# Attention values written transposed in 32-column groups: no evacuation, no transposes back, sums from a block of ones

## The reference

```python
    x = x + _L0_xattn_ref(_layernorm(x, axis=-1), ctx_1024, ctx_1024, mask_BxS2_bk0, ...)
    x = x + _L0_ffn_ref(_layernorm(x, axis=-1), L0_ffn_wg1, L0_ffn_bg1, L0_ffn_wg2, L0_ffn_w_in, L0_ffn_w_out)
...
        qh, kh, vh = (split_heads(qp), split_heads(kp), split_heads(vp))
        scores = jnp.einsum('bhqd,bhkd->bhqk', qh, kh) * d_head ** (-0.5)
        ...
        attn = jax.nn.softmax(scores, axis=-1)
        out = jnp.einsum('bhqk,bhkd->bhqd', attn, vh)
        out = out.transpose(0, 2, 1, 3).reshape(b, l, d_model)
        return out @ Wo.T + bo
```

## Time and profile before

| | us |
|---|---|
| median of three runs | 765.07 |
| the profiled execution, its own time | 765.94 |
| its span, first to last instruction | 763.8 |
| attention, up to the last `values` | about 454 |
| expert stage | about 460 to 720 |
| tail | about 720 to 764 |

### The profile page before, as it was taken

One profiled execution on the slowest core, in us unless ns is written; L12 is line 12 of the kernel. 1 busy time (PEld: TensorE's weight loads), 2 busy tenths in 40 slices (PEclk: granted clock), 3 DMA queues, 4 the chain that ended last, 5 costly groups with the idle time before them and its releaser, 6 DMA issues.

```text
span 763.8 us, 14153 instructions
## 1 busy us (share of the span) xinstructions
PE 574.9 (75%) x4326; PEld 405.7 (53%) x4326; DVE 443.1 (58%) x1706; ACT 407.7 (53%) x862; POOL 359.7 (47%) x438
## 2 busy tenths in 40 slices
PE   3499999889888988898898767483778866789800
PEld 1156666556455555555465446362667755679700
DVE  4267788778777877777785773251323322223374
ACT  2257988887787888688786655230322322224300
POOL 4122126644554564455435326647555555550075
PEclk9989999999999999999998987867898999989955
DMA  3363111221122122201111224324544444446498
GB/s 89 71 195 84 45 41 44 61 67 43 50 60 66 29 65 63 66 24 30 38 29 32 83 59 122 105 77 112 158 133 124 118 125 124 120 131 186 133 364 291
DMA packets 74458, 73.59 MB, mean 96 GB/s; under 512 B 22032, under 2 KB 61840, under 8 KB 74096
## 3 DMA queue, kind: packets, MB, share of 16 engines
q1 hardware_dynamic: 64160, 53.86, 26.8%
q0 software_dynamic: 8640, 18.37, 6.8%
q10 hardware_dynamic: 1584, 0.46, 0.2%
HBM read 44.99 MB, written 27.70 MB: 95 GB/s over the span
## 4 chain that ended last, share of the span: by engine, by line
PE 53%; ACT 14%; issue 13%; DVE 7%; another core or an unknown queue 4%; POOL 4%; SPq 2%; DMA 2%; ACTq 0%; POOLq 0%; DVEq 0%
PE bank L638 12%; PE bank L649 10%; PE bank L462 6%; PE bank L484 6%; DVE sm L890 3%; PE bank L466 3%; POOL gathered L1417 3%; PE bank L475 3%; PE bank L629 3%; ACT sm L717 2%; ACT pt L782 2%; ACT vx L709 2%; ACT rows L744 2%; PE bank L491 2%
## 5 line engine op out<-in xcount | busy, mean ns | idle before, releaser
L1354 POOL DMA_INDIRECT routed_rows<-rows,pos x128 | 125.2, 978 | 136.4 <-ACT rows L746 86.2
L1390 POOL DMA_INDIRECT expert_rows_by_token<-yb,token_row x118 | 113.2, 960 | 85.7 <-DVE token_row L1248 40.8
L638 PE MATMUL bank<-xbT,wi 128*128 128x256 f32 x312 | 97.1, 439 | 71.1 <-issue 70.4
L827 ACT ACTIVATE hb<-bank 128x512 f32<-128x512 f32 x78 | 46.6, 597 | 168.7 <-PE bank L638 77.4
L1254 DVE TENSOR_TENSOR yb<-bank,gate 128x256 f32<-128x256 f32 x78 | 33.1, 424 | 172.2 <-PE bank L649 107.2
L638 PEld LDWEIGHTS bank<-xbT,wi 128*128 128x128 f32 x312 | 59.6, 212 | 84.7 <-issue 77.0
L882 DVE TENSOR_REDUCE smax<-bank 128x8 f32<-128x512 f32 x128 | 82.2, 683 | 30.7 <-PE bank L466 25.4
L649 PE MATMUL bank<-wo,hb 128*128 x624 | 91.6, 295 | 0.0
L649 PEld LDWEIGHTS bank<-wo,hb 128*128 128x128 f32 x624 | 85.3, 212 | 0.1
L462 PE MATMUL bank<-kx,qT 64*64 64x512 f32 x512 | 74.6, 654 | 14.0 <-DMA kx<-kT 7.1
L890 DVE TENSOR_TENSOR sm<-bank,smax 128x512 f32<-128x512 f32 x128 | 81.9, 681 | 0.0
(11 more groups left out here) (135 smaller groups left out, 934.8 us busy)
## 6 DMA issues: line engine op xcount, KB each, us to landing
xb<-routed_rows SPq DMA_DIRECT2D x78, 138.0 KB
wi<-w_in SPq DMA_DIRECT2D x78, 128.0 KB
kx<-expert_rows_by_token SPq DMA_DIRECT2D x26, 256.0 KB
ctx_in<-ctx_t SPq DMA_DIRECT2D x16, 256.0 KB
x_all<-x SPq DMA_DIRECT2D x16, 256.0 KB
kx<-kT SPq DMA_DIRECT2D x256, 16.0 KB
out<-x_all SPq DMA_DIRECT2D x16, 256.0 KB
expert_rows<-yb SPq DMA_DIRECT2D x19, 128.0 KB, 2.1
```

What stands on the lines that cost most here:

```text
L638: last = nc.tensor.matmul(UBK[b % 2][:, c * BLK:(c + 1) * BLK], wi[:, b % RX, c * P:(c + 1) * P], xbT[:, b % RH, :], start=True, stop=True)
L1354: nc.gpsimd.indirect_dma_start(out=rows_d, out_offset=bass.IndirectOffsetOnAxis(ap=pos[:, buf, k, u:u + 1], axis=0), in_=rows[:, buf, u, : ...
L1390: nc.gpsimd.indirect_dma_start(out=tok_d, out_offset=bass.IndirectOffsetOnAxis(ap=token_row[:, b % RY, u:u + 1], axis=0), in_=yb[:, b % RY ...
```

## The change

- `vx` becomes double by group, and each pair of adjacent value pairs lies in one row of 160 columns with zeros between, so that a window of 32 columns picks the features of one head pair for one sequence, at the place where they belong among 32 output partitions.
- `values` makes 16 matmuls of 32 stationary columns and 64 queries: for each half of a head group (j), each sequence (b) and each of four column groups (g). The four column groups write four different quarters of the partitions of `XB[:, 0:128]`. Nothing is computed for the wrong sequence. Eight more matmuls (32 columns, 128 queries) with a constant block of ones put the sum of each head on all eight of its features' partitions in `XB[:, 128:256]`.
- DVE's `normalise` takes the reciprocal of 128 x 128 sums and multiplies once, straight into `onT`, which is now double. There are no `xo`, `on`, `queries_to_rows`, `transpose_o` and `onT_evac`.
- `values(t)` newly waits for `normalise(t - 1)`, because it overwrites `XB`; `project_o(t - 1)` waits for it too. The waits that stood before `queries_to_rows` move to just before `project_o`. `v_evac` waits for an older tile's values only.
- At the start one memset of `vx` (5120 numbers per partition) takes the place of four copies of 512. The gathers of the tail use 8 buffers inside `sm` in place of 6 of their own.

```diff
-        vx = sb("vx", [P, U, J, VM])
+        vx = sb("vx", [P, 2, U * J // 2, 2, 2 * VB + 2 * DH])
...
                 def values(t, u):
+                    if t:
+                        pe.wait_ge(s_norm, t)
                     pe.wait_ge(s_ptev, 2 * t + 2)
-                    for j in range(J):
-                        o = VM * (j % 2)
-                        last = nc.tensor.matmul(XB[o:o + VM, (j // 2) * P:(j // 2 + 1) * P], vx[:, u, j, :],
-                                                pt[:, j, :], start=True, stop=True)
+                    for j in range(2):
+                        for b in range(2):
+                            for g in range(J // 2):
+                                v = vx[:, t // U % 2, u * (J // 2) + g, :, :].rearrange("p a c -> p (a c)")
+                                c = (2 * j + b) * VB
+                                nc.tensor.matmul(XB[g * VB:(g + 1) * VB, b * L:(b + 1) * L], v[:, c:c + VB],
+                                                 pt[:, 2 * g + j, b * L:(b + 1) * L], start=(j == 0 and b == 0), stop=False,
+                                                 skip_group_check=True)
+                    for j in range(2):
+                        for g in range(J // 2):
+                            last = nc.tensor.matmul(XB[g * VB:(g + 1) * VB, P:2 * P],
+                                                    ones_s[:, j * VB:(j + 1) * VB], pt[:, 2 * g + j, :],
+                                                    start=False, stop=(j == 1), skip_group_check=True)
                     last.then_inc(s_pv, 1)
-                def queries_to_rows(t):
-                    pe.wait_ge(s_xev, t + 1)
...
-                def transpose_o(t):
...
                 def project_o(t):
-                    pe.wait_ge(s_ontev, t + 1)
-                    nc.tensor.matmul(YB[:, P:2 * P], onT[:, :], wo_s[:, :], start=True, stop=True).then_inc(s_y, 1)
+                    if t:
+                        pe.wait_ge(s_res, t)
+                    pe.wait_ge(s_norm, t + 1)
+                    nc.tensor.matmul(YB[:, 0:P], onT[:, t % 2, :], wo_s[:, :], start=True, stop=True).then_inc(s_y, 1)
...
                 def v_evac(s):
                     act.wait_ge(s_v, s + 1)
+                    if runs(s, 2):
+                        act.wait_ge(s_pv, (s - 1) * U)
...
-                        act.wait_ge(s_pv, t + 1)
-                        nc.scalar.activation(xo[:, :, :].rearrange("p c q -> p (c q)"), XB[:, :], ACT.Copy
-                                             ).then_inc(s_xev, 1)
...
                 def normalise(t):
-                    dve.wait_ge(s_tq, t + 1)
-                    y = YB[:, :].rearrange("r (j m) -> r j m", m=VM)
-                    nc.vector.reciprocal(rden[:, :, :], y[:, :, 4 * DH:4 * DH + 2]).then_inc(s_rden, 1)
+                    if t > 1:
+                        dve.wait_ge(s_y, t - 1)
+                    dve.wait_ge(s_pv, t + 1)
+                    nc.vector.reciprocal(rden[:, :], XB[:, P:2 * P]).then_inc(s_rden, 1)
                     dve.wait_ge(s_rden, t + 1)
-                    for b in range(2):
...
-                    last.then_inc(s_norm, 1)
+                    nc.vector.tensor_tensor(onT[:, t % 2, :], XB[:, 0:P], rden[:, :], ALU.mult).then_inc(s_norm, 1)
...
-                for u in range(U):
-                    last = nc.vector.tensor_copy(vx[:, u, :, :], ones_s[:, :].unsqueeze(1).broadcast_to([P, J, VM]))
-                last.then_inc(s_zero, 1)
+                nc.vector.memset(vx[:, :, :, :, :], 0.0).then_inc(s_zero, 1)
```

More of the change, by code:

```diff
@@ L31 @@
 EPS = 1e-5
-VM = 64
+VB = 32
 J = H // 2
@@ L61 @@
 RL = 2 * HH // KTOP
-RG = 6
+RG = 8
 TB0 = SPS[0] * U
@@ L95, in build @@
     spread_c = nc.inline_tensor((NEG_B * np.eye(P)).astype(np.float16), name="mask_spread")
-    ones_cols = np.zeros((P, VM), np.float32)
-    for p in range(2):
-        ones_cols[p * L:(p + 1) * L, 4 * DH + p] = 1.0
+    ones_cols = np.zeros((P, 2, VB), np.float32)
+    for j in range(2):
+        for p in range(2):
+            o = (2 * j + p) * DH
+            ones_cols[p * L:(p + 1) * L, j, o:o + DH] = 1.0
+    ones_cols = ones_cols.reshape(P, 2 * VB)
     ones_c = nc.inline_tensor(ones_cols, name="value_ones")
@@ L558, in body @@
                         transpose_probs(t, u)
-                        if before:
-                            if u > 1 or runs(s, 1):
-                                pe.wait_ge(s_res, t - 1)
-                            if u == 2 and runs(s, 2):
-                                pe.wait_ge(s_lsh, s - 1)
-                            if u == 0 and runs(s, 3):
-                                pe.wait_ge(s_pch, 6 * s - 16)
-                            queries_to_rows(t - 1)
                         if u == 0 and runs(s, 0, NS - 2):
@@ L585, in body @@
                             transpose_rows(s - 2, par)
-                        if before:
-                            transpose_o(t - 1)
                         if u == 3 and runs(s, 0, NS - 2):
@@ L604, in _ @@
                     body(s, s // 2, s % 2)
-                pe.wait_ge(s_res, NT - 1)
-                pe.wait_ge(s_pos, NS - 2)
-                queries_to_rows(NT - 1)
                 transpose_rows(NS - 2, 0)
-                transpose_o(NT - 1)
                 gate_hidden(NS - 2)
-                pe.wait_ge(s_ontev, NT)
+                pe.wait_ge(s_pch, 6 * NS - 16)
                 project_o(NT - 1)
```

52 lines of the change are left out of this document (19 added, 33 removed).

## The result

The kernel after takes 806.71 us (median of 4; 802.29 to 810.34), beside 764.15 for the kernel before in the same job: ratio 1.0574, 95% interval 1.0521 to 1.0626. The forecast was 725. Two later jobs gave 1.0583 (1.0468 to 1.0698) and 1.0575 (1.0486 to 1.0663).

A forecast was written before the change was run, and what follows sets the result against it. Bound by a DVE-PE loop, ACT's stream and a hold once a group, no engine full. Gains 33 (groups 4 to 13) + 6 + 4 = 43, less 2, 41 us: 765.94 - 41 - 0.9 = 724, said as 725; range 716 to 734.

The forecast's parts named there:

- the hold: Once a group ACT and DVE wait on something remote; taken from first `pt` start to release, 5.9 us on average.
- And the hold: Release at 17.2 + 5.9 = 23.1 us still ends last, so a group's period goes from 26.4 to 23.1 us.
- rivals 2 and 3: The hold's release doesn't move with ACT's rows, 742 us (0.09); or the hold goes away, 703 us (0.07).
- rival 4: Slower: the 24 matmuls don't run side by side or issue too slowly; values 2.75 us, total 800 us; chance 0.07.
- The values on PE: New values and ones block on PE: 1.03 to 1.47 us a tile, taken as 1.05, about 1.03 before.
- rival 1: First half: 64-query passes no shorter, values 1.47 us; second: DVE's reciprocal 1.0 us. Either 736 to 740, both 748; chance 0.16.
- DVE: `normalise` on DVE: reciprocal taken as 0.65 us, whole 0.95 (0.6 to 1.3) against 0.89 before: no gain.
- Rival 2: The hold's release doesn't move with ACT's rows: 1.7 us won behind `project_v` lost, 17 in ten groups, 742; chance 0.09.
- The loop without holds: Path through DVE and PE over one group: the first projection would end at 20.9 us, before the hold's release.
- Groups 0 to 3: No hold there, PE without a gap: 0.6 us won in two or three tiles, 1.5 a group, 6 in all.

The follow-up runs named there:

- align: Kernel after, with POOL's row scatters of turns 1 and 2 waiting for that turn's values to be reported: 766.40 us, ratio 1.0036.
- b_recip: Kernel before, with an extra reciprocal of 128 x 128 numbers on DVE in each tile, into a spare buffer: 765.85 us, ratio 0.9999.
- split0: As align, and turn 0's four scatters cut into two pairs, the second behind the turn's values: 727.78 us, ratio 0.9451; again 0.9396.
- spread3_2: Rerun of kernel after with one scatter pair behind turn 0's values, one behind turn 1's, four behind turn 2's: 729.79 us, ratio 0.9589.
- run8: Kernel after, with all eight row scatters of a group issued in one run in turn 0: 833.46 us, ratio 1.0887.
- probe2: Separate program, second run: TensorE blocks beside 0 to 8 indirect scatters; first values block's report 4.8 us late with four, on time with none.
- b_s0_split16: Kernel before, row scatters moved behind the values blocks and its 8 products of values cut into 16: 652.46 us, ratio 1.0081; repeat (_2) 739.74 us, 0.9693.

## Why the prediction was wrong

The step that failed is the hold: "I take it as an interval from the group's first `pt` start to the release", and then, in *And the hold*, "The hold lets go at 17.2 + 5.9 = 23.1". It took one hold a group, at a fixed place, and asked only whether its end would move or it would vanish (rivals 2 and 3). It didn't ask what makes it, though it names the condition: it begins with POOL's scatters. The new block puts three times the instruction rows into the turns in which POOL issues its other two pairs. There the runs showed a second hold of 1.9, half clock for 1.4 and a values block 1.6 longer, all of it gone from these turns in align. No rival had a second hold, and rival 4, which ends on the right side, did so by another mechanism.

The path against the trace, with 0 at 257.77:

| | forecast | after | what lies between |
|---|---|---|---|
| scores, u = 1 | 1.53 | 1.55 | right |
| values | 3.00 | 3.11 | right |
| values and ones on PE | 1.05 | 1.02 | right |
| residual | 4.82 | 6.75 | a hold, 1.9 |
| scores, u = 2 | 6.68 | 8.72 | same |
| values, u = 2 | 8.15 | 11.60 | half clock, 1.4 |
| residual | 9.76 | 14.81 | values 2.68 for 1.05, 1.6 |
| next `pt` | 17.2 | 22.25 | same |
| release of turn 0 | 23.1 | 29.86 | also 7.6 after `pt`, not 5.9 |

The numbers behind the second half are 272.58 for the second residual, 280.02 for `pt`, 287.63 for the next residual after the hold:
```profile
272.58 0.29 DVE L890 TENSOR_TENSOR x_all<-bank,x_all 128x128 f32<-128x128 f32 x1 [2.14 <-PE bank L502]
...
287.63 0.29 DVE L890 TENSOR_TENSOR x_all<-bank,x_all 128x128 f32<-128x128 f32 x1 [2.62 <-remote]
```
```profile
280.02 1.08 ACT L772 ACTIVATE pt<-bank 128x512 f32<-128x512 f32 x2
```
```profile
281.72 0.98 POOL L1331 DMA_INDIRECT routed_rows<-rows,pos  x1 [9.50 <-DVE pos L971]
```
Every late entry lies behind a hold, the clock that falls after one, or the values that stand still beside a run. Up to the next `pt` that is 5.1; of the 1.7 of the last line 1.5 comes by POOL: its run started 0.18 after `pt` before, with ACT's rows, and 1.70 after it now, because DVE's positions come last.

*The values on PE*: right, and rival 4 and the first half of rival 1 with it wrong. The 24 matmuls take 1.02, on average 0.043 us each. The estimate of 1.49 in the prediction went by the Trainium skill's "TensorE: Matmul & The Clock Gate", section "Wait — 56ns, not 53.3ns?", whose 62 ns a MATMUL hold with hardware decode off; the trace doesn't have them, and no run tells which way of decoding was on.

*DVE*: the reciprocal took 0.94 on average where 0.65 was taken and 1.0 was the bound; `normalise` 1.17 (259.46 to 260.63) instead of 0.95. The slope between the two rows in sight was the wrong ruler, and it was misread: 0.04 / 12 is 0.0033, which gives 0.59, not 0.64. The steeper slope of the bound, 0.08 / 12, was near: 0.94 / 128 is 7.3 ns a number. The Trainium skill's "VectorE: DVE Perf Modes", section "First, the fixed hardware budget", gives the reciprocal's divide a repeat count of 8; the trace has 0.94 beside the 0.29 of a multiplication as large, 3.2 times, which fits a dearer instruction but doesn't show the count. That the reciprocal cost nothing is shown in the kernel before (b_recip); for the kernel after no run tells.

*Rival 2* took 1.7 for what is won behind `project_v`. By the prediction's own numbers it is 5.96 before (20.47 - 14.51) and 4.44 after (17.2 - 12.76), so 1.5.

*The loop without holds* was put at 20.9 a group. split0 shows 23.64, with DVE busy 277.62 of 300, that is 21.9 a group. So 20.9 was below what DVE's work alone takes; 4 x 0.22 of it is the reciprocal. A forecast for split0 by this path would have been too low by some 2.7 a group, and that 725 is near 728 is chance.

*Groups 0 to 3*: 6 us forecast, 7.1 measured (136.31 to 129.18). Right in size: 0.7 is there before the first values, then the groups win 2.2, 1.4, 2.1 and 0.6, where 1.5 each was forecast. The reason given, a PE without a gap, fits the kernel before (from 70 to 130 us PE busy 56.38 of 60). After, DVE is the fuller one (PE 54.22, DVE 55.14), so there part of PE's gain may be used up by DVE; no run parts the two.

## What to carry to other kernels

Where a profile has waits "on remote" or "on issue" that end just after a run of indirect DMAs, take them as a resource that PE's short instructions share with that run: list every run and what PE does in it, before and after the change, turn by turn. An edit that makes one matmul into three can be cheap on PE and cost 4 us a group by where it falls. And it is worth moving the runs on purpose: behind the report of the block with the most short instructions, which here took 79 of 807 us off the changed kernel and 3.8% off the one before. Then look again at what the moved run meets (in spread3_2 the projection of the values), and whether anything waits for it.

## What was not expected of the hardware

- TensorE's reports come up to 8.4 us after the modelled end of their work (run8) while GpSimd issues indirect scatters of 0.96 us each, and TensorE itself is slowed to one to six matmul rows in 0.7 us (probe2). VectorE's and ScalarE's work and reports go on meanwhile (in the kernel after DVE runs its maxima from 261.41 to 262.68, POOL being at its first scatter).
- One of the seven jobs ran on a chip that had none of it, with the same 0.96 for a scatter, and had the kernel before in 648 us where the others took 760 to 773. On it the attention of b_s0_split16 had a period of 24.21 a group, and 24.59 on the chip of b_s0_split16_2. From the last values to the end it took 228.9 there and 313.6 here, 85 of the 90 us between the two. In that part POOL scatters the experts' rows, and the kernel before waits 69.3 us in 15 waits on remote for the first product of the experts alone (its longest is 13.7):
```profile
ACT hb L827 <- remote: 69.3, 15, 13.7
```
- Moving the scatters of the attention leaves that part as it was: split0, too, has 51.0 us of such waits of ACT and 58.5 of DVE. No run moved the scatters there, so that they cause these waits is not shown.
- What differs between these chips is not known, and no run tells it. Nor does a run tell whether it is POOL's issuing that does it or the traffic that it starts, or whether the recording of every instruction takes part.
